# Layer 0: ScalarE's two convolution products of a slot moved behind the decays of states 2 and 3

## What is computed

```python
x  = hs @ in_proj_w.T                                   # 768 -> 1536 channels
xs = conv3x3_depthwise(x, conv_w) + conv_b              # pad 1
u  = xs * sigmoid(xs)
dt, Bs, Cs = split(u @ x_proj_w.T)                      # 48, 4, 4
delta  = softplus(dt @ dt_w.T + dt_b)
states = scan(exp(delta * A), delta * u * Bs)           # along the 4096 positions
y = sum_n states_n * Cs_n + D * u
out = layernorm(y) @ out_proj_w.T
```

## Time and profile before

| | |
|---|---|
| median of 3 runs | 3728.86 us (3728.01 to 3731.64) |
| the profiled execution | 3728.46 us |
| its span, first to last instruction | 3726.7 us |
| PE busy | 3406.2 us (91%) |
| DVE busy | 2914.2 us (78%) |
| ACT busy | 2353.8 us (63%) |
| POOL busy | 2344.5 us (63%) |
| mean granted TensorE clock | 0.955 |

### The profile page before, as it was taken

How to read it: one execution, slowest core, us unless ns; L and a number is a source line. 1 busy time by engine, 2 the same in 40 slices (tenths; PEclk the granted TensorE clock), 3 DMA queues, 4 the chain that set the end, 5 groups by cost and what they waited for, 6 DMA issues and landing times. The chain is left out here.

```text
span 3726.7 us, 39056 instructions
## 1 busy us (share of the span) xinstructions
PE 3406.2 (91%) x10696; PEld 1733.7 (47%) x10696; DVE 2914.2 (78%) x4082; ACT 2353.8 (63%) x4095; POOL 2344.5 (63%) x1557
## 2 busy tenths in 40 slices
PE   4876799999999999999999999998798999999999
PEld 4432233333333344333333333333235877777787
DVE  4469999999999979999999999999754346566532
ACT  1357777887778757777877778787535556543211
POOL 0149888989889878898988888899850001112211
PEclk7887899999999999999999999999898999999999
DMA  7244455555556544555555555554643223356664
GB/s 284 89 140 109 103 131 139 158 141 146 136 142 157 149 122 122 147 141 140 157 144 146 136 141 150 145 156 113 165 98 115 66 71 111 118 189 211 206 200 153
DMA packets 217034, 529.85 MB, mean 142 GB/s; under 512 B 24728, under 2 KB 45784, under 8 KB 213872
## 3 DMA queue, kind: packets, MB, share of 16 engines
q1 hardware_dynamic: 173808, 376.32, 31.8%
q0 software_dynamic: 43008, 151.02, 18.6%
HBM read 346.11 MB, written 80.48 MB: 114 GB/s over the span
## 5 line engine op out<-in xcount | busy, mean ns | idle before, releaser
L564 PE MATMUL p_in<-xn,win_v 128*128 128x512 f32 (+1 forms) x2304 | 1064.9, 611 | 102.9 <-ACT halo L747 64.6
L580 PE MATMUL p_op<-uy,wout_ring 128*128 128x512 f32 x2160 | 1020.1, 622 | 83.7 <-DVE x_res L952 83.5
L917 DVE TENSOR_TENSOR_SCAN p_da<-p_da,state,g_ring 128x512 f32<-128x512 f32 x672 | 827.1, 1276 | 110.4 <-ACT p_da L706 74.7
L889 POOL TENSOR_TENSOR g_ring<-du,B_bc 128x2048 f32<-128x2048 f32 x192 | 870.6, 4534 | 17.3 <-DMA B_bc<-bc_scratch 2.4
L938 DVE SCALAR_TENSOR_TENSOR p_cv<-win_v,conv_w,p_cv 128x512 f32<-128x512 f32 x960 | 722.7, 753 | 88.0 <-ACT p_cv L768 67.0
L564 PEld LDWEIGHTS p_in<-xn,win_v 128*128 128x128 f32 x2304 | 443.1, 197 | 697.5 <-issue 697.5
L580 PEld LDWEIGHTS p_op<-uy,wout_ring 128*128 128x128 f32 x2160 | 413.4, 198 | 680.4 <-issue 568.3
L706 ACT ACTIVATE p_da<-delta,A 128x512 f32<-128x512 f32 x768 | 499.4, 682 | 12.6 <-ACT state L711 0.2
L923 DVE TENSOR_TENSOR g_ring<-p_da,C_bc 128x512 f32<-128x512 f32 x768 | 486.7, 675 | 0.0
L1366 PE MATMUL banks<-x_split,w_split 128*128 128x512 f32 x1152 | 459.2, 399 | 11.9 <-DVE x_split L1569 6.5
L1368 PE MATMUL banks<-x_split,w_split 128*128 128x512 f32 x1152 | 450.8, 391 | 0.0
(11 more groups left out here) (213 smaller groups left out, 4261.1 us busy)
## 6 DMA issues: line engine op xcount, KB each, us to landing
g_ring<-g_ring POOLq DMA_DIRECT2D x192, 512.0 KB, 5.5
win_v<-in_win SPq DMA_DIRECT2D x192, 384.0 KB, 3.1
wout_ring<-wout_scratch SPq DMA_DIRECT2D x184, 384.0 KB, 4.0
x_ring<-x_scratch SPq DMA_DIRECT2D x192, 256.0 KB, 2.7
q_scratch<-q_ring POOLq DMA_DIRECT2D x96, 256.0 KB, 2.5
x_split<-q_scratch SPq DMA_DIRECT2D x96, 256.0 KB, 3.4
out<-x_ring POOLq DMA_DIRECT2D x96, 256.0 KB, 2.9
x_res<-in_x SPq DMA_DIRECT2D x90, 256.0 KB, 4.6
```

What stands on the lines that cost most here:

```text
L564: last = nc.tensor.matmul(p_in[:, 0:n], WR[:, i % NW, t, :], XN[:, t, off:off + n], start=(t == 0), stop=(t == XT - 1))
L580: last = nc.tensor.matmul(p_op[:], OR[:, e % NO, k - h * HALF, :], ucol(c * K + k), start=(k == 0), stop=(k == K - 1))
L889: nc.gpsimd.tensor_tensor(G[:, i % NG], DU[:].unsqueeze(1).broadcast_to([P, NS, N]), BB[:], ALU.mult).then_inc(s_dbu, 1)
L917: nc.vector.tensor_tensor_scan(bank, bank, G[:, i % NG, n, :], init, ALU.mult, ALU.add)\
```

## The change

The two calls of `product` in ScalarE's loop body move. Before, product 0 stood ahead of u times D, and product 1 behind it, both ahead of the decays of states 2 and 3. After, both stand together behind these decays, ahead of `load_norm`, of SiLU and softplus and of the evacuation. No instruction is added or removed, the waits of each instruction are the same, and no other engine's program changes.

```diff
                         nc.scalar.activation(XD[:], p_dt[:, 0, :], ACT.Copy).then_inc(s_xe, 1)
-                    if b is not None:
-                        product(b, 0)
                     i = tile(S, L_SCAN)
                     if i is not None:
                         act.wait_ge(s_du, i + 1)
                         nc.scalar.activation(ucol(i), ucol(i), ACT.Copy, scale=Dp[:, i % K:i % K + 1])\
                           .then_inc(s_skip, 1)
-                    if b is not None:
-                        product(b, 1)
                     c = chunk_at(S, S_XP[2] + 1)
                     if c is not None:
                         act.wait_ge(s_xf, c + 1)
...
                         decay(i, 2)
                         decay(i, 3)
+                    if b is not None:
+                        product(b, 0)
+                        product(b, 1)
                     if S % K == 0 and S < NT:
                         load_norm(S // K)
```

## The result

The changed kernel takes 3816.28 us (median of 4 runs, 3812.42 to 3819.20) where the kernel before takes 3729.62: a ratio of 1.0231, with a 95% interval of 1.0214 to 1.0249. The forecast was 3810 in a range of 3778 to 3838. The profiled execution took 3816.15 us with a span of 3814.4, so 87.7 us more than the profiled one before; the sum said 81.

The account below looks back on a forecast made before the run. VectorE bounds plain slots, the chain through ScalarE the SiLU and softplus slots. Losses of 58.3 (ten regular blocks), 13.0, 8.7 and 1.2 sum to 81 us over the profiled 3728.5: 3810 us, range 3778 to 3838.

Parts of the forecast that it names:

- the sum: Whole kernel: losses of regular blocks 58.3, blocks 7 and 15 13.0, 1 and 2 8.7, 8 1.2; total 81 us.
- The bound: Layer 0: VectorE bounds plain slots; in SiLU and softplus slots the chain runs through ScalarE, with little slack.
- The price, 1.22 us for two products side by side: ScalarE's queue behind the decays: two overlapped products take 1.22 us, or 1.43 if nothing overlaps.
- The slack of each slot: Regular block: slack reduces the 1.22 us, leaving losses of 0.77 at position 7, 1.19 at 10, 0.21 at 11.
- rival 3: All slots: products still fill ScalarE's idle time, so no change, 3729 us; chance 0.04.
- What is hidden beside what: Position 2's loss of about 1.2 us runs beside TensorE's 1.22 from position 0, seen at position 3; nothing more.
- The sum for a regular block: Losses at positions 0, 3, 6, 7, 10 and 11 sum to 5.83 us a block, 58.3 for ten.
- The other blocks: Blocks 7 and 15 lose 13.0 us together, 1 and 2 8.7, block 8 1.2, block 0 nothing.
- The clock: TensorE's longer gaps at positions 0 and 3 may lower its clock, slowing the matmuls behind them; left to rival 1.
- rival 1: Clock falls in TensorE's gaps: 2.8 us at position 0, about 1 at position 3; 3833 to 3855 us; chance 0.13.
- Rivals 2 to 4: TensorE paces blocks, 3781 or 3766, chance 0.13; no change, 3729, 0.04; faster, 3719 at best, 0.02.
- B: Theory for the experiments: TensorE paces the blocks and takes up the SiLU losses; SiLU-only within 8 us of before.

Follow-up runs that it names:

- SiLU-only kernel: Products behind the decays only in the SiLU slots (positions 2, 6, 10), against the kernel before: 3753.78 us, ratio 1.0066.
- the fill at position 0 alone: Two extra products of constants in TensorE's gap, added to the kernel with products moved only at position 0: 3742.40 us, ratio 1.0040 against the kernel before.

## Why the prediction was right

- **The bound.** That the chain runs through ScalarE in the SiLU and softplus slots and at position 0, and nowhere else, was right: moving the products in the five plain slots changed nothing (0.9997), and the SiLU slots (25.1 us), the softplus slots (32.2) and position 0 (26.2) give 83.5 us one by one, of some 87 together.
- **The price, 1.22 us for two products side by side**. Position 7 waits 1.62 in place of 0.37 and position 4 3.27 in place of 2.01: 1.25 and 1.26. Right; the bound of 1.43 was not needed.
- **The slack of each slot.** Position 7's loss was put at 0.77, and the wait at position 8 is 0.73; position 10's at 1.19, and the wait at position 11 is 1.14. Position 11's was put at 0.21, and little of it is there: position 0 waits 0.73 us in place of 0.6 to 0.8. Under rival 3 the prediction says that the rows show a slack of 0.03 to 0.35 us. By its own list it is 0.45 at position 7 (1.22 less 0.77) and 1.01 at position 11, which changes nothing in the sum.
- **What is hidden beside what.** Position 2's loss beside TensorE's path to position 3 was right: in the SiLU-only kernel that wait shrank from 2.15 to 0.91, and with position 0 moved too it is back at 2.15 in the changed kernel, behind the 1.14 us of position 2's loss. Likewise position 0 was right as a path: without it a regular block is at 161.7, with it at 163.0.
- **The sum for a regular block** was 5.83, measured 5.8 where the twelve matmuls at position 0 take 5.39 us.
- **The other blocks** were sized less well. Blocks 7 and 15 cost about 6 (160.1 against 154.1 us between two marks), not 6.5. Blocks 1 and 2 were put at 8.7; up to the first mark, at position 8 of block 2, 5.2 had come together (481.2 against 476.0), and that mark varies by itself: in the kernel with the plain slots moved, which is as fast as before, it is at 472.0. Block 8 was put at 1.2, and the period that spans it is 182.4 against 177.8: 4.6. There three input projections take about 7 us in the profile after, where before one took 8.06 and one 6.28; what of the 4.6 this is was not tried apart.
- **The clock.** The forecast left it out of the likeliest case and gave it 0.13. It came, at 1.7 us instead of 2.8 a time and in five blocks of the ten regular ones: some 8 us. The errors of the other blocks, 3.5 us too much for blocks 1 and 2, 1.1 too much for 7 and 15, 3.4 too little for block 8, nearly cancel, which is luck, so the 6.7 us between the sum and the profiled time are about the clock's. The step that was too small is this one, as a term: a gap was to be counted as sometimes costing, not as one case or the other. Ahead of the result the two gaps of the earlier trace rows, with the clock of the earlier trace rows, were all that spoke for and against it at this length; that idle time there costs more than itself was the author's estimate, and the fill at position 0 alone agrees with it (3754.87 without, 3742.40 with). No row ahead of the result shows the 1 us of rival 1 for the dt products: it is an estimate, and with only the softplus slots moved four second pairs of ten at position 3 took 1.37 to 2.08 us in place of 1.13.
- **Rivals 2 to 4** fell: B by the SiLU-only kernel, no change and faster by the result. ScalarE did lose its waits for GpSimd, 6.5 us of them, and it brought nothing, since they lay in idle time.

## What to carry over

Idle time of an engine that waits for a partner at a fixed point is a place, not an amount: work put ahead of that wait is free as far as it fits in, and the same work behind it lengthens the chain, here by 1.22 us less the slot's slack, even if the engine is busy only 63% of the time. Before an instruction is moved past a wait, walk the chain from the wait to the next instruction that the bounding engine needs, slot kind by slot kind, and subtract each slot's slack. And ask which queued instruction feeds another engine first: here moving that one, the norm, ahead of the wait gained 10.6 us.

## What the runs showed of the hardware

Behind gaps of one length TensorE's granted clock was down in some blocks and not in others, within one execution. In the changed kernel, after 2.16 us of idling, twelve matmuls took 7.08 or 5.39 us (granted clock 0.77 to 0.80, or 1.00). With only the softplus slots moved, behind 2.13 to 2.14 us at position 3, the second dt pair took 2.08 us in one regular block (2186.03 us) and 1.13 in another (732.30 us, granted clock 1.00). In the kernel before, behind 0.85 to 0.97 us at position 0 and 0.88 us at position 3, they took 5.39 and 1.13 us in all ten regular blocks. But the length of the last gap doesn't decide alone. In block 0, where twelve matmuls of 64 columns (1.52 us, behind a gap of 0.95 us ahead of the first row and 1.07 ahead of the second) stand between two gaps, the changed kernel has both outcomes behind 0.49 us, at a granted clock of 1.00 and 0.76:

```profile
124.75 5.39 PE L564 MATMUL p_in<-xn,win_v 128*128 128x512 f32 x12 [0.49 <-ACT win_v L722]
...
133.22 7.08 PE L564 MATMUL p_in<-xn,win_v 128*128 128x512 f32 x12 [0.49 <-ACT win_v L722]
```

So in these kernels a wait on TensorE's path that grew from 0.96 to 2.16 us at position 0 cost more than its own length in some of its instances, 1.69 us more in the changed kernel. Filling it with products that nobody uses gained 12 us in one kernel (3754.87 to 3742.40) and nothing in another (3814.78 and 3815.28).

Behind the gap of 4.04 us at position 9 the twelve matmuls took 8.02 to 8.40 us in nine blocks of the kernel before and 6.85 to 8.47 in nine of the kernel with only position 0 moved. From the latter:

```profile
1125.47 8.47 PE L580 MATMUL p_op<-uy,wout_ring 128*128 128x512 f32 x12 [4.04 <-DVE x_res L956]
...
1937.68 6.85 PE L580 MATMUL p_op<-uy,wout_ring 128*128 128x512 f32 x12 [4.04 <-DVE x_res L956]
```

In the first the granted clock is 0.50 from 1125.5 to 1130 us and 0.59 from 1130 to 1132; in the second it is 0.50 from 1937.7 to 1940 us and 0.85 from 1940 to 1942. In the block of the first row VectorE waits 1.05 us at the next position 0, in that of the second not at all. In this kernel every burst of 8.25 us and more behind this gap has a wait of 0.8 to 1.05 us after it, the one of 8.21 has 0.27, and those of 7.12 and 6.85 us have none. So in these blocks the wait at position 0, which a working by rows takes for a fixed lack of slack, went with the length of the slow burst three positions earlier.
